# Two stage joins of a two-layer kernel: negated maxima and weight tiles made one block earlier, sums sent one block later

## The reference

```python
def L0_attn(x, w_q, w_k, w_v, w_o):
    q, k, v = (proj(w) for w in (w_q, w_k, w_v))      # (batch, 32 heads, 512, 16)
    scores = einsum('bhqd,bhkd->bhqk', q, k) / sqrt(16)
    out = einsum('bhqk,bhkd->bhqd', softmax(scores), v)
    return einsum('bse,oe->bso', out, w_o)
def L0_ffn(x, gate_w, up_w, down_w, gs, us, ds):
    inter = silu(x @ gate_w.T * gs) * (x @ up_w.T * us)
    return inter @ down_w.T * ds
xn = layernorm(x)
x = x + L0_attn(xn, ...) + L0_ffn(xn, ...)
xn = layernorm(x)
x = x + L1_attn(xn, ...) + L1_ffn(xn, ...)            # SSM block, low-rank linear layer
```

## Time and profile before

| | us |
|---|---|
| timed runs, median (lowest to highest) | 2262.8 (2262.0 to 2267.0) |
| the profiled execution's own time | 2265.07 |
| its span | 2263.1 |
| TensorE busy in it | 2116.1 |
| VectorE, ScalarE, GpSimd busy | 1469.1, 1374.9, 885.5 |
| mean granted clock of TensorE, share of full speed | 0.975 |

### The profile page before, as it was taken

One profiled execution on the slowest core, in us unless ns is written; L12 is line 12 of the kernel. 1 busy time (PEld: TensorE's weight loads), 2 busy tenths in 40 slices (PEclk: granted clock), 3 DMA queues, 4 the chain that ended last, 5 costly groups with the idle time before them and its releaser, 6 DMA issues. The chain is left out here.

```text
span 2263.1 us, 37073 instructions
## 1 busy us (share of the span) xinstructions
PE 2116.1 (94%) x12040; PEld 1566.3 (69%) x12040; DVE 1469.1 (65%) x1813; ACT 1374.9 (61%) x2396; POOL 885.5 (39%) x758
## 2 busy tenths in 40 slices
PE   6889999898699999999999999999999977999998
PEld 5634444476587777777777777777777755888886
DVE  4446666274468777778778687677778664555555
ACT  2145555433378888888788788788788762333222
POOL 0011111130147666667667566575766670000000
PEclk9989999998899999999999999999999997999999
DMA  4422222232335545445454455455455546444462
GB/s 132 157 79 69 77 72 62 75 125 60 93 115 174 160 154 157 151 146 164 148 163 155 126 179 158 132 159 159 140 167 158 166 165 244 142 141 141 141 213 75
DMA packets 184055, 310.81 MB, mean 137 GB/s; under 512 B 20512, under 2 KB 96800, under 8 KB 183744
## 3 DMA queue, kind: packets, MB, share of 16 engines
q1 hardware_dynamic: 183872, 308.53, 43.6%
HBM read 252.52 MB, written 55.68 MB: 136 GB/s over the span
## 5 line engine op out<-in xcount | busy, mean ns | idle before, releaser
L145 PE MATMUL ssm_pp<-xhi,ssm_lo 128*128 128x512 f32 x1192 | 482.9, 405 | 34.4 <-issue 15.2
L147 PE MATMUL ssm_pp<-xhi,ssm_hi 128*128 128x512 f32 x1192 | 469.8, 394 | 0.0
L146 PE MATMUL ssm_pp<-xlo,ssm_hi 128*128 128x512 f32 x1192 | 469.5, 394 | 0.0
L1413 ACT ACTIVATE ssm_sct<-ssm_cumb,ssm_gpar 128x128 f32<-128x128 f32 x1024 | 313.0, 390 | 57.3 <-DMA ssm_cumb<-dt_sums 49.7
L1508 DVE SCALAR_TENSOR_TENSOR ssm_xc<-ssm_pp,vectors,ssm_xc 128x1022 f32<-128x1022 f32 (+2 forms) x192 | 245.3, 1278 | 125.4 <-ACT ssm_xc L1374 110.5
L137 POOL TENSOR_TENSOR ssm_lo<-ssm_raw,ssm_hi 128x512 fp32r<-128x512 f32 x149 | 263.1, 1770 | 111.0 <-ACT ssm_hi L126 110.9
L145 PEld LDWEIGHTS ssm_pp<-xhi,ssm_lo 128*128 128x128 f32 x1192 | 226.4, 190 | 102.1 <-issue 34.3
L147 PEld LDWEIGHTS ssm_pp<-xhi,ssm_hi 128*128 128x128 f32 x1192 | 226.4, 190 | 49.0
L146 PEld LDWEIGHTS ssm_pp<-xlo,ssm_hi 128*128 128x128 f32 x1192 | 226.5, 190 | 43.7
L1543 DVE TENSOR_TENSOR ssm_sct<-ssm_sct,ssm_cbm 128x1024 f32<-128x1024 f32 x128 | 228.3, 1783 | 34.4 <-ACT ssm_sct L1420 19.2
L1674 POOL TENSOR_TENSOR ssm_go<-ssm_t,ssm_gt 128x512 f32<-128x512 f32 x128 | 164.6, 1286 | 177.0 <-DVE ssm_t L1579 112.8
(11 more groups left out here) (210 smaller groups left out, 4028.3 us busy)
## 6 DMA issues: line engine op xcount, KB each, us to landing
ssm_cumb<-dt_sums SPq DMA_DIRECT2D x96, 1024.0 KB, 6.3
ssm_raw<-w SPq DMA_DIRECT2D x149, 256.0 KB, 2.7
gated<-ssm_go SPq DMA_DIRECT2D x128, 256.0 KB, 4.9
out_graw<-gated SPq DMA_DIRECT2D x64, 512.0 KB, 4.2
out_raw<-w SPq DMA_DIRECT2D x65, 256.0 KB, 2.7
ssm_cumb<-dt_sums SPq DMA_DIRECT2D x32, 512.0 KB, 4.5
ffn_raw<-w SPq DMA_DIRECT2D x37, 256.0 KB, 2.8
stk_qs<-qk_parts SPq DMA_DIRECT2D x96, 64.0 KB, 2.2
```

Source lines behind the costliest of these rows:

```text
L145: pe.matmul(out, wlo, xhi, start=start, stop=False)
L146: pe.matmul(out, whi, xlo, start=False, stop=False)
L147: return pe.matmul(out, whi, xhi, start=False, stop=stop)
L1413: i = act.activation(sct[:, s % 2, h, :], cumb[:, s % 2, 0, h, :], ACT.Relu, scale=-1.0, bias=gpar[:, unit, 0, s % NTOK, h:h + 1])
```

## The change

- `turn`, `high`, `low` and `neg_max` become methods of `Stacks`. Unit 0's are done in the projections' block: turn, high and low at step t = 4 of the v steps (`HELD`), the transfers by SyncE after its last parts. The transpose writes into a part of `qkv_ps` that is free then.
- The first two gate/up weight tiles are loaded and split in that block too (`next_feed`).
- The last unit's sums are sent to memory at the head of the down stage (`move_sums`), no longer at the end of attention. Their buffer `oe` is now part of the raw buffers of the SSM weights' feed.
- h's splits (`Hidden`) lie in the memory of the stacks `qs` and `ks`, which live on to the end of the down stage. The splits of h's tiles 0 and 1 are made in attention's last unit, by ScalarE after exponentials 6 and 8 and by VectorE in steps 4 and 5. The splits of the attention output's last two quarters lie there as well.
- In the down stage `a_high` stands one tile later (3, 5, 7, 9), and `h_high` and `h_low` start with tile 2.

```diff
+class Hidden:
+    def __init__(self, nc, ctx, h, qs, ks):
+        ...
+        part = lambda x: x[:].rearrange("p n j t -> p n (j t)")
+        self.hi, self.lo = part(qs), part(ks)
+    def high(self, act, k):
+        act.activation(self.hi[:, k % 2, :], self.h[:, k, :], ACT.Copy).then_inc(self.hi_done, 1)
+    def low(self, dve, k):
+        dve.wait_ge(self.hi_done, k + 1)
+        dve.tensor_tensor(self.lo[:, k % 2, :], self.h[:, k, :], self.hi[:, k % 2, :].bitcast(F32), ALU.subtract
+                          ).then_inc(self.lo_done, 1)
 # emit_qkv
+        ptr = ps[:, 2, 0, :]
+        HELD = NTOK // 2
         def _(pool):
             st.clear(pool)
+            next_feed.begin_lo(pool)
         # sync, after the last parts
+            next_feed.begin_load(sp)
+            st.neg_max(sp, 0, 0)
             for i, s in enumerate(parts_out):
         # tensor, after the row steps of t
+                if t == HELD:
+                    st.turn(pe, c, ptr, 0, 0)
         # scalar, after the copy of v's step t
+                if t == HELD:
+                    st.high(act, ptr, 0, 0)
+                    next_feed.begin_hi(act)
         # vector, after maximum(i, u)
+                    if (i, u) == (1, 1):
+                        st.low(dve, ptr, 0, 0)
 # emit_attention, sync
-            feed.begin_load(sp)
             for n in range(feed.begun, 5):
                 feed.load(sp, w, W_FFN + n, 0, n)
             sweep(sp, body)
-            out(NIT - 1, NB - 1)
             weights(NIT - 1, NB - 1, True)
 # tensor
-            turn(0, 0)
 # vector, end of step k, and before the sweep
+                        if last and i == NB - 1 and k in (4, 5):
+                            hid.low(dve, k - 4)
-            low(0, 0)
 # scalar, before the sweep, and after exps(it, i, u)
-            high(0, 0)
-            feed.begin_hi(act)
+                        if last and i == NB - 1 and u in (6, 8):
+                            act.wait_ge(key_sum, NQUAD * 16 - 2 * 16)
+                            hid.high(act, u // 2 - 3)
 # emit_down, sync, at its head
+            move_sums(sp, c, oe, att_moved, NIT - 1, NB - 1)
             for s in att_moved:
                 sp.wait_ge(s, NQUAD // 2 * 2 * HQ * 16)
             attention(0)
 # scalar
-            h_high(0)
             for k in range(FT):
-                if k + 1 < FT:
+                if 0 < k < FT - 1:
                     h_high(k + 1)
                 ...
-                if k in (2, 4, 6, 8):
+                if k in (3, 5, 7, 9):
                     a_high(k // 2 - 1)
 # vector
-            h_low(0)
             for k in range(FT):
-                if k + 1 < FT:
-                    h_low(k + 1)
+                if 0 < k < FT - 1:
+                    hid.low(dve, k + 1)
```

More of the change, by code:

```diff
@@ L265, in __init__ @@
         self.stacked = [sem(f"stacked{i}") for i in range(NB)]
[L266 to L267 removed]
+        self.qs, self.ks = qs, ks
         self.vs = sb("vs", [P, 2, NC, HQ, 32])
         self.v = sb("v", [P, NTOK, D])
+        self.neg_hi, self.neg_lo = sem("neg_hi"), sem("neg_lo")
+        self.max_in = [sem(f"max_in{i}") for i in range(NB)]
+        self.nmh = sb("nmh", [HQ * 4, 2, P], F32R)
+        self.nml = sb("nml", [HQ * 4, 2, P], F32R)
         self.mx = sb("mx", [P, 2, HQ * 4])
@@ L311, in maximum, with turn, high, low @@
                           ).then_inc(self.max_done, 1)
+    def turn(self, pe, c, ptr, it, i):
+        n = it * NB + i
+        pe.wait_ge(self.neg_done, n + 1)
+        after(pe, self.neg_lo, n)
+        pe.transpose(ptr[0:HQ * 4, 0:P], self.nm[:, i % 2, :], c.ident[:]).then_inc(self.neg_t, 1)
+    def high(self, act, ptr, it, i):
+        n = it * NB + i
+        act.wait_ge(self.neg_t, n + 1)
+        if not isinstance(it, int) or it > 0 or i >= 2:
+            act.wait_ge(self.max_in[(i + 2) % NB], (it + (0 if i < 2 else 1)) * 4 * 16)
+        act.activation(self.nmh[:, i % 2, :], ptr[0:HQ * 4, 0:P], ACT.Copy).then_inc(self.neg_hi, 1)
+    def low(self, dve, ptr, it, i):
+        n = it * NB + i
+        dve.wait_ge(self.neg_hi, n + 1)
+        if not isinstance(it, int) or it > 0 or i >= 2:
+            dve.wait_ge(self.max_in[(i + 2) % NB], (it + (0 if i < 2 else 1)) * 4 * 16)
+        dve.tensor_tensor(self.nml[:, i % 2, :], ptr[0:HQ * 4, 0:P], self.nmh[:, i % 2, :].bitcast(F32),
+                          ALU.subtract).then_inc(self.neg_lo, 1)
+    def neg_max(self, sp, it, i):
+        n = it * NB + i
+        sp.wait_ge(self.neg_lo, n + 1)
+        for r, src in ((0, self.nmh), (1, self.nml)):
+            for half in range(2):
+                at = half * HALF + KSTACK + r
+                sp.dma_start(self.qs[at:at + 1, i, :, :].bitcast(F32)
+                             .rearrange("o j (q t) -> o (j q) t", q=4),
+                             src[half * 8:half * 8 + 8, i % 2, :].bitcast(F32)).then_inc(self.max_in[i], 16)
     def negate(self, dve, it, i):
@@ L503, in _ @@
         def _(sp):
[L504 to L512, removed]
-            def out(it, i):
[L515 to L522, removed]
+            def out(it, i):
+                sp.wait_ge(out_copied, it * NB + i + 1)
+                move_sums(sp, c, oe, out_moved, it, i)
             def weights(it, i, last):
@@ L549, in _ @@
         def _(pe):
[L550 to L553, removed]
-                pe.transpose(ptr[0:HQ * 4, 0:P], nm[:, i % 2, :], c.ident[:]).then_inc(neg_t, 1)
             def key_step(it, i, u):
@@ L603, in body @@
                         if k == 1 and not (last and i == NB - 1):
-                            turn(*step(it, i, 1))
+                            st.turn(pe, c, ptr, *step(it, i, 1))
                         if k == 0 and i > 0:
@@ L617, in _ @@
         def _(dve):
-            def low(it, i):
-                n = it * NB + i
-                dve.wait_ge(neg_hi, n + 1)
-                if not isinstance(it, int) or it > 0 or i >= 2:
-                    dve.wait_ge(max_in[(i + 2) % NB], (it + (0 if i < 2 else 1)) * 4 * 16)
-                dve.tensor_tensor(nml[:, i % 2, :], ptr[0:HQ * 4, 0:P], nmh[:, i % 2, :].bitcast(F32),
-                                  ALU.subtract).then_inc(neg_lo, 1)
             def out(it, i):
@@ L657, in body @@
                         if k == 3 and not (last and i == NB - 1):
-                            low(*step(it, i, 1))
+                            st.low(dve, ptr, *step(it, i, 1))
                         if k == 7 and not (last and i >= NB - 2):
@@ L677, in _ @@
         def _(act):
-            def high(it, i):
-                n = it * NB + i
-                act.wait_ge(neg_t, n + 1)
-                if not isinstance(it, int) or it > 0 or i >= 2:
-                    act.wait_ge(max_in[(i + 2) % NB], (it + (0 if i < 2 else 1)) * 4 * 16)
-                act.activation(nmh[:, i % 2, :], ptr[0:HQ * 4, 0:P], ACT.Copy).then_inc(neg_hi, 1)
             def exps(it, i, u):
@@ L823, in h_high @@
             def h_high(k):
-                after(act, tile_done, FIRST + k - 1 if k >= 2 else 0)
-                act.activation(h_hi[:, k % 2, :], h[:, k, :], ACT.Copy).then_inc(h_hi_done, 1)
+                act.wait_ge(tile_done, FIRST + k - 1)
+                hid.high(act, k)
             def a_high(k):
                 act.wait_ge(normed, k + 1)
-                act.activation(a_hi[:, k, :], parts(k)[:, 0, :], ACT.Copy).then_inc(a_hi_done, 1)
+                act.activation(weighted(k)[0], parts(k)[:, 0, :], ACT.Copy).then_inc(a_hi_done, 1)
             def o_high(k):
```

64 lines of the change are left out of this document (37 added, 27 removed).

## The result

The changed kernel's median is 2237.7 us over 4 runs (2236.1 to 2239.1), against 2262.4 (2261.2 to 2267.0) for the kernel before on the same chip: ratio 0.9887, 95% interval 0.9870 to 0.9904. The forecast was 2236.0. The profiled execution took 2239.05 us, its span is 2237.1, forecast 2238.3 and 2236.3.

What follows compares the result with a forecast made beforehand. TensorE, busy 94% of the span, was taken as the bound, the down stage's end hanging on VectorE's last a_low. Gains 12.5 + 14.3 = 26.8 us from 2265.07 gave 2238.3 profiled, 2236.0 timed; range 2230 to 2243.

Steps and rivals of the forecast that it cites:

- Join 1, transfer and weights: Projections to attention: without the wait for maxima and weights, first key step at about 112.3 instead of 123.77, gain 11.5 us.
- Join 1, clock: After the projections-to-attention gap: low clock costs 1.6 us instead of 2.7, 1.0 us of gain counted, bounds 0 and 2.
- The insert in the last unit: ScalarE's two Copies in attention's last unit: TensorE loses 0.95 us, bounds 0 and 2.
- Join 2: Attention to down stage: TensorE starts tile 0 at 430.7, 5.57 us earlier, with no clock drop.
- Down stage: VectorE's four waits go, 8.3 us; x lands at 496.8 against 511.06, gain 14.3 us together with attention's end.
- the two meetings: First two GpSimd splits of the down stage run into VectorE's two-operand instructions, costing 0.95 us each.
- Behind the addition of x: After x arrives at the down stage's end: no clock change counted, bounds -0.5 and +1.6 us.
- The signs: Key step within 1 us of release, down product within 2.5, first reciprocal's wait 1 to 3, x about 26 us earlier.
- 1 (more meetings): Down stage: three or four more splits meet VectorE's two-operand instructions, x load 4 to 5 us later, 2241; chance 0.17.
- Rival 3: Down stage keeps its old pace, 8.3 us of idleness returns as waits, gain 18.5 us, 2244.5; chance 0.11.
- Rival 4: TensorE's clock stays low through the down stage, 52 us over 11 tiles, 2288; chance 0.02.
- rival 2: No meetings in the first two tiles, no clock drop at projections-to-attention or behind x: 2231.5; chance 0.13.

Runs made afterwards that it cites:

- e5c: Changed kernel with the first maxima's turn, splits and transfers back at the head of attention, only the two weight tiles early: 2241.2 us, ratio 0.9906.
- e6c: Changed kernel with the first two weight tiles loaded and split at the head of attention again, only the maxima early: 2241.5 us, ratio 0.9901.
- e10: Changed kernel with both the maxima's work and the first two weight tiles back at the head of attention: 2246.1 us, ratio 0.9924.
- e9: Kernel before with only SyncE's order changed: the maxima's four transfers go ahead of the two weight loads that wait for splits: 2259.2 us, ratio 0.9978.
- The repeats: Two further measurements of the changed kernel with no edit: 2236.5 us each, ratio 0.9881 each.
- e2c: Changed kernel with the last unit's eight transfers of sums back at the end of attention: 2242.9 us, ratio 0.9915.
- e3: Changed kernel with h's tiles 0 and 1 split at the head of the down stage again: 2240.8 us, ratio 0.9897.
- e1_order_back: Changed kernel with ScalarE's a_high back at down-stage tiles 2, 4, 6, 8: 2248.3 us, ratio 0.9927.
- e4: Changed kernel with the two early high splits behind exponentials 5 and 9 instead of 6 and 8: 2236.6 us, ratio 0.9881.
- e7: Changed kernel with ScalarE's weight split ahead of h_high in the down stage: 2234.2 us, ratio 0.9879.

## Why the prediction was right, and where its terms were off

- **Join 1, transfer and weights: right.** Forecast 11.5 us to the first key step at 112.3; measured 11.2 at 112.57, or 11.8 from the block's release. e5c, e6c and e10 show both inputs to be needed, e9 that half of it was queue order.
- **Join 1, clock: the mis-sized term.** I took a low stretch of 3.4 us, from the stretch after a gap of 2.10 us, and counted a gain of 1.0. The stretch was 6.8 us, longer than the 5.5 after nearly 15 us of idleness, and the term came out at -0.5 (11.2 shrinks to 10.7 by the third step). The repeats have the same 6.8 us, so it isn't one trace's chance. One row at another place was no price for this one.
- **The insert in the last unit: right in its wait (0.80 us, forecast 0.95).** The profiled trace lost 2.5 us from the third step's sums to the last ones, 297.00 to 299.49 us; 0.8 is the wait and 1.7 a clock drop behind it (0.50 in 411 to 412). The two repeats have the wait without the drop, so the drop isn't a price that this change pays each time.
- **Join 2: right.** The distance from last sums to first product fell from 8.76 to 2.31 us, 6.45 against 6.5 forecast. e2c and e3 show each of its two waits alone.
- **Down stage: right in mechanism and nearly in size.** The first product to the addition of x went from 74.79 to 64.73 us, 10.1 against 8.7. The four waits of 2.07 went, the wait for the sums was 1.76 (forecast 1.9), and the two meetings fell where laid out, at 0.91 and 0.93 us each (forecast 0.95). The 1.4 us more: x was sent 56.4 us behind the first product and not 56.9, since TensorE had none of the waits that I gave it and VectorE stood still nowhere between its first reciprocal and its last `a_low`; and x took 8.3 us to arrive instead of 9.2.
- **Behind the addition of x.** I counted nothing, with +1.6 as a bound; 1.8 us came, and it is the clock's. TensorE waited 1.05 us before its first turn instead of 2.92, but that wait itself gains nothing here, since the turn starts 2.80 us behind the addition in both traces. Behind the 2.92 us the clock had been low, as in e1_order_back behind 2.64; behind the 1.05 it is 1.00 throughout. The kernel before:
```profile
515.00:517.00 2.00, 2.00 (x6) 1.56 (x6) 1.50 (x5) 0.45 (x2) 0.00 (x0) 0.51 0.00 0
517.00:519.00 2.00, 2.00 (x8) 1.53 (x8) 0.10 (x1) 0.00 (x0) 0.00 (x0) 0.64 0.00 0
```
- **Layer 1:** 1716.5 us before, 1717.1 after. Nothing, as forecast.
- **The signs.** The key step came 0.3 us behind the release, the first down product 2.31 behind the last sums, the wait before the first reciprocal was 1.76, and no even `low` had idle time before it. x was sent 23.9 us earlier and not 26 in the profiled execution, mostly for the two clock terms of join 1 and the last unit, and 26.6 and 26.7 earlier in the repeats.

In sum 10.7 - 2.5 + 6.5 + 10.1 + 1.8 - 0.5 = 26.0 (to rounding), against 26.8. The clock terms missed in both directions and nearly cancelled, so that the sum is as close as this is partly luck; the mechanism of each part is what the experiments bear out. The Trainium skill (TensorE: Matmul & The Clock Gate, "What's actually happening") has the watching run freely against a kernel's work; the traces agree, since the same wait of 0.80 us at the same place was followed by a drop in one execution of this kernel and by none in the two repeats.

Of the rivals, 1 (more meetings) didn't occur: every later two-operand instruction of the stage takes 1.15 to 1.23 us. The Trainium skill (SBUF — State Buffer, "Who interferes with whom") names the exclusion behind them, and this case agrees: VectorE's instructions of 1.2 us took 2.12, 2.14 and 2.15 us, each ending about 1.1 after GpSimd's, and in e1_order_back GpSimd's 1.29 became 2.33. Rival 3 (only the joins pay) is refuted by e1_order_back: with ScalarE's old order 8.3 us of the stage are lost again. Rival 4 fails with the windows of the changed kernel; the clock is 1.00 in every stretch of ten from 430 to 500 us, and in the middle of the stage TensorE and VectorE are both full:
```profile
460.00:470.00 10.00, 10.00 (x45) 7.91 (x43) 9.97 (x6) 4.22 (x5) 2.57 (x2) 1.00 0.81 288
```
Of rival 2's three terms one came (no drop behind x, 1.8 us); both meetings took place, and at join 1 the clock was low for longer, not shorter.

## What to carry to other kernels

Follow the end of a stage back over all engines: a stage in which TensorE is busy was ended by a load that VectorE released, and the cure was one tuple in ScalarE's order. Ask of every queue at a block's head which of its transfers is ready and which waits, and send the ready ones first; that was worth 4 to 5 us of 2263 by itself. When a join has two late inputs, work out each alone as well: removing one uncovers the other, and here each alone gained about half of the whole.

## What the hardware showed beyond the forecast

The granted clock after a gap can't be priced from its length here: a gap of 2.85 us brought 6.8 us of low clock in all three traces of this kernel, one of 0.80 us brought 3.3 us of it in one execution and none in two, and 1.24 us at join 2 brought none. These three traces differ by 2.75 us at attention's end, 1.7 of it for that reason and 1.0 from the projections' block, ahead of the change. Small edits of under 2 us (e4, e7) were plain in the rows and not to be told in the times.

Which engine pays when VectorE's two-operand instruction and GpSimd's split meet hangs on a fraction of a microsecond: with GpSimd 0.14 to 0.25 us ahead VectorE took 2.1 to 2.2 us, and with both starting within 0.02 us GpSimd took 2.33. An edit that moves one engine moves the meetings to other tiles, as e2c and e1 show.
